# A macaron block on one NeuronCore: the attention output product as three fp32r passes, its input split on ScalarE and VectorE, and the bias sums on GpSimd moved

## The reference

```python
x = x + 0.5 * ffn(norm(x))          # first half step
x = x + attn(norm(x))               # RWKV time mix and channel mix
x = x + 0.5 * ffn(norm(x))          # second half step
# ffn: weighted sum of 8 chosen 256x256 adapters and their biases
# inside attn, on its own input a:
h = layernorm(a, ln1);  hh = h shifted by one token
xk, xv, xr = h * tm + hh * (1 - tm)
k, v, sr = xk @ Wk.T, xv @ Wv.T, sigmoid(xr @ Wr.T)
rwkv = sr * wkv(time_decay, time_first, k, v)   # a scan over tokens
a = a + rwkv @ Wo.T                              # the output product
h = layernorm(a, ln2);  hh = h shifted by one token
kk = square(relu(xck @ Wck.T))                   # keys, 1024 wide
a + sigmoid(xcr @ Wcr.T) * (kk @ Wcv.T)          # gate times values
```

## Time and profile before

| what | value |
|---|---|
| median of 3 runs | 431.5 us (431.36 to 431.73) |
| the profiled execution | 431.73 us, span 429.9 us |
| TensorE matmul busy | 417.1 us, 97% |
| TensorE weight loads busy | 337.0 us, 78% |
| VectorE busy | 367.9 us, 86% |
| ScalarE busy | 329.7 us, 77% |
| GpSimd busy | 185.6 us, 43% |
| granted TensorE clock | 1.000 over the span |

### The profile page before, as it was taken

How to read it: one execution, slowest core, us unless ns; L and a number is a source line. 1 busy time by engine, 2 the same in 40 slices (tenths; PEclk the granted TensorE clock), 3 DMA queues, 4 the chain that set the end, 5 groups by cost and what they waited for, 6 DMA issues and landing times.

```text
span 429.9 us, 6308 instructions
## 1 busy us (share of the span) xinstructions
PE 417.1 (97%) x2042; PEld 337.0 (78%) x2042; DVE 367.9 (86%) x725; ACT 329.7 (77%) x669; POOL 185.6 (43%) x194
## 2 busy tenths in 40 slices
PE   8989989889999999999999999999999999999996
PEld 8865875568868887798769886888779876988985
DVE  2988989998989999998989998999999898886235
ACT  1157977899799969997899979997999489945420
POOL 1446052727272635635372728263553347033011
PEclk9999999999999999999999999999999999999999
DMA  6992010001000110002000200010000000000101
GB/s 200 376 398 81 2 49 0 0 2 52 0 0 2 57 44 0 0 26 74 2 0 25 74 1 2 0 50 1 2 0 25 26 0 2 25 26 0 50 2 50
DMA packets 15972, 18.52 MB, mean 43 GB/s; under 512 B 1083, under 2 KB 13635, under 8 KB 15939
## 3 DMA queue, kind: packets, MB, share of 16 engines
q1 hardware_dynamic: 14538, 17.05, 11.4%
q10 hardware_dynamic: 1400, 1.07, 0.8%
HBM read 13.92 MB, written 4.19 MB: 42 GB/s over the span
## 4 chain that ended last, share of the span: by engine, by line
PE 77%; DVE 1%; issue 0%; ACT 0%; DVEq 0%
PE pair L484 22%; PE pair L362 10%; PE pair L374 10%; PE pair L458 6%; PE pair L459 6%; PE pair L462 6%; PE pair L352 6%; PE pair L343 4%; PE pair L499 3%; PE pair L428 1%; PE pair L432 1%; PE pair L429 1%; PE pair L514 0%; DVE rwkv L1054 0%; DVE work L1048 0%
## 5 line engine op out<-in xcount | busy, mean ns | idle before, releaser
L484 PE MATMUL pair<-wcv_sb,kk 128*128 128x256 f32 x448 | 100.4, 380 | 0.0
L484 PEld LDWEIGHTS pair<-wcv_sb,kk 128*128 128x128 f32 x448 | 83.8, 190 | 11.3 <-ACT kk L741 0.7
L458 PE MATMUL pair<-xck_hi,wck_hi 128*128 128x512 f32 x128 | 54.4, 425 | 0.0
L462 PE MATMUL pair<-xck_lo,wck_hi 128*128 128x512 f32 x128 | 50.7, 396 | 0.0
L459 PE MATMUL pair<-xck_hi,wck_lo 128*128 128x512 f32 x128 | 50.6, 395 | 0.0
L737 ACT ACTIVATE kk<-pair 128x512 f32<-128x512 f32 x64 | 36.3, 589 | 14.2 <-PE pair L462 13.3
L1349 POOL TENSOR_TENSOR x2b<-xs,bias_bc 128x512 f32<-128x512 f32 (+1 forms) x16 | 21.8, 1364 | 56.6 <-DVE xcr_lo L1127 22.9
L1349 POOL TENSOR_TENSOR x<-x,bias_bc 128x512 f32<-128x512 f32 x14 | 18.1, 1296 | 55.7 <-DVE rwkv L1054 36.3
L741 ACT ACTIVATE kk<-kk 128x512 f32<-128x512 f32 x64 | 35.9, 625 | 0.0
L1389 POOL TENSOR_TENSOR xs<-x,xa 128x512 f32<-128x512 f32 x16 | 20.4, 1273 | 31.6 <-DVE xa L1060 31.0
L1309 POOL TENSOR_TENSOR rstd_x<-vare_x,nhalf 128x4 f32<-128x4 f32 (+2 forms) x26 | 27.3, 1050 | 9.1 <-DVE vare_x L909 7.8
(11 more groups left out here) (173 smaller groups left out, 1119.3 us busy)
## 6 DMA issues: line engine op xcount, KB each, us to landing
x<-in_x_dram SPq DMA_DIRECT2D x8, 512.0 KB, 4.0
out_dram<-xs SPq DMA_DIRECT2D x15, 256.0 KB, 2.1
xt<-in_xt_dram SPq DMA_DIRECT2D x4, 512.0 KB, 8.2
work<-in_ffn_w_dram ACTq DMA_DIRECT2D x4, 256.0 KB, 5.1
work<-in_ffn_w_dram SPq DMA_DIRECT2D x4, 256.0 KB, 5.2
kk<-in_wck_dram SPq DMA_DIRECT2D x1, 1024.0 KB, 9.6
xs<-in_xt_dram SPq DMA_DIRECT2D x2, 512.0 KB, 10.8
wcv_sb<-in_wcv_dram SPq DMA_DIRECT2D x1, 1024.0 KB, 12.5
```

Of the source, the lines that this page charges most:

```text
L458: nc.tensor.matmul(key_bank(n), wck_hi[:, h, cols], xck_hi[:, h, :], start=h == 0, stop=False)
L462: last = nc.tensor.matmul(key_bank(n), wck_hi[:, h, cols], xck_lo[:, h, :], start=False, stop=h == CH - 1)
L484: last = nc.tensor.matmul(bank_of("kv", e, i)[:, t % TB * C:(t % TB + 1) * C], kk[:, n, tok:tok + P], wcv_sb[:, n, :], start=n == 0, stop= ...
```

## The change

For batches 1 to 7 the output product runs through `three_passes`. Its weight is split once at the start (`wo_hi`, `wo_lo`), its input for each batch: `rwkv_hi` is a copy on ScalarE, `rwkv_lo` a difference on VectorE. TensorE now waits for `rwkv_lo` and not for `rwkv`, and the product stands behind six of the eight matmuls of `channel_values(e, 0)` in place of four. On ScalarE the copies stand behind square 5, the residual behind them, then squares 6 and 7, and the channel gate last. On VectorE the two differences stand around the first half of `add_second`. On GpSimd the two sums into `x1` both wait for the denominators (`den_done`) and no longer for the scan `aa` and for `rwkv`. Of the sums into `x2b`, the one that stood first waits for `xcr_lo`, and the other moves to the end of the iteration before, behind `xcr`. The values of the last batch (`last_values`) are three passes as well, with their keys and weight split.

```diff
             def output_product(f):
                 if f == 0:
                     pe.wait_ge(s_wo, 1)
-                pe.wait_ge(rwkv_done, 2 * f + 2)
-                to_tokens("o", rwkv, wo_sb, xa2_done, f, o_ps)
+                    pe.wait_ge(rwkv_done, 2 * f + 2)
+                    to_tokens("o", rwkv, wo_sb, xa2_done, f, o_ps)
+                    return
+                if f == 1:
+                    pe.wait_ge(s_wo_lo, 1)
+                pe.wait_ge(rwkv_lo_done, 2 * (f - 1) + 2)
+                for i in range(BANKS):
+                    take(pair_of("o", f), i, xa2_done, 2 * f + i + 1)
+                    for t in range(TB):
+                        last = three_passes(bank_of("o", f, i)[:, t * C:(t + 1) * C], i * TB + t, rwkv_hi, rwkv_lo, wo_hi, wo_lo)
+                    last.then_inc(o_ps, 1)
...
                 for n in part:
+                    high = wcv_hi[n // (HB // 2)][:, n % (HB // 2), :]
                     if t == 0:
-                        pe.wait_ge(sq_done, HB * LAST + n + 1)
-                    last = nc.tensor.matmul(by_tiles(last_bank(LAST_KV, j), j)[:, t - LAST_PARTS[j][0], :], kk[:, n, t * P:(t + 1) * P], wcv_sb[:, n, :],
-                                            start=n == 0, stop=n == HB - 1)
+                        pe.wait_ge(kk_hi_done, n + 1)
+                    nc.tensor.matmul(dst, kk_hi[:, n, tok], high, start=n == 0, stop=False)
+                    nc.tensor.matmul(dst, kk_hi[:, n, tok], wcv_lo[:, n, :], start=False, stop=False)
+                    if t == 0:
+                        pe.wait_ge(kk_lo_done, n + 1)
+                    last = nc.tensor.matmul(dst, kk_lo[:, n, tok], high, start=False, stop=n == HB - 1)
...
-                channel_values(e, 0, range(HB // 2))
+                channel_values(e, 0, range(HB - 2))
                 if has(f):
                     output_product(f)
-                channel_values(e, 0, range(HB // 2, HB))
+                channel_values(e, 0, range(HB - 2, HB))
...
+            def output_input_high(f):
+                act.wait_ge(r_ps, 2 * f + 2)
+                for h in range(CH):
+                    act.wait_ge(rwkv_done, 2 * f + h + 1)
+                    nc.scalar.activation(rwkv_hi[:, h, :], rwkv[:, h, :], ACT.Copy).then_inc(rwkv_hi_done, 1)
...
+            def output_input_rest(f, h):
+                dve.wait_ge(rwkv_hi_done, 2 * (f - 1) + h + 1)
+                nc.vector.tensor_tensor(rwkv_lo[:, h, :], rwkv[:, h, :], rwkv_hi[:, h, :].bitcast(F32), ALU.subtract).then_inc(rwkv_lo_done, 1)
...
+                if has(f):
+                    output_input_rest(f, 0)
                 if has(e - 1):
                     add_second(e - 1, 0)
+                if has(f):
+                    output_input_rest(f, 1)
...
                 if has(e - 1):
+
+                    pool.wait_ge(xcr_lo_done, 2 * e + 2)
                     bias_to_x2(e - 1, 1)
                 if e - 1 >= SUMS_X2:
                     inverse_std("x2", e - 1)
-                if has(e - 1):
-
-                    pool.wait_ge(xcr_lo_done, 2 * e + 2)
-                    bias_to_x2(e - 1, 0)
...
-                    pool.wait_ge(aa_done, 2 * f + 2)
+                    pool.wait_ge(den_done, 2 * f + 2)
                     bias_to_x(f + 1, 0)
-                    pool.wait_ge(rwkv_done, 2 * f + 2)
                     bias_to_x(f + 1, 1)
```

More of the change, by code:

```diff
@@ L148, in build @@
         rwkv = sb("rwkv", [P, CH, T])
+        rwkv_hi, rwkv_lo = in_place_of("xr", "rwkv_hi", [P, CH, T]), in_place_of("rwkv", "rwkv_lo", [P, CH, T])
         xv_hi, xv_lo = in_place_of("thr", "xv_hi", [P, CH, T]), in_place_of("xv", "xv_lo", [P, CH, T])
@@ L381, in ffn_setup @@
                 pe.wait_ge(s_bias_sel, 16 * K)
-                nc.tensor.matmul(pair[0][:, 0, 0:C], gate_rows[:, :], bias_sel[:, :], start=True, stop=True).then_inc(s_bias_ps, 1)
+                nc.tensor.matmul(pair[0][:, 0, 0:C], gate_rows[:, :], bias_sel, start=True, stop=True).then_inc(s_bias_ps, 1)
                 pe.wait_ge(s_ffn_acc, K)
@@ L385, in ffn_setup @@
                     for h in range(CH):
-                        last = nc.tensor.matmul(pair[0][:, 1, a * C:(a + 1) * C], (centre_own if a == h else centre_other)[:, :], ffn_sum[:, h, :],
+                        last = nc.tensor.matmul(pair[0][:, 1, a * C:(a + 1) * C], (centre_own if a == h else centre_other), ffn_sum[:, h, :],
                                                 start=h == 0, stop=h == CH - 1)
@@ L874, in _ @@
                     key_square(e, n)
+                for n in range(HB // 2, HB - 2):
+                    key_square(e, n)
+                if has(f):
+                    output_input_high(f)
+                    residual_of(f)
+                for n in range(HB - 2, HB):
+                    key_square(e, n)
                 channel_gate(e)
[L876 to L879, removed]
                 if has(f + 1):
@@ L888, in _ @@
                     past_cr(f)
+            key_relu(LAST, 4)
+            for n in range(HB - 5):
+                last_key_parts(n)
+                key_relu(LAST, n + 5)
+            for n in range(HB - 5, HB):
+                last_key_parts(n)
+            channel_gate(LAST)
             for j in range(len(LAST_PARTS)):
@@ L1174, in last_bias, with last_weight_rest, last_key_rest @@
                                         bias_bc[:, :].rearrange("p (a c) -> p a c", a=1).broadcast_to([P, len(LAST_PARTS[j]), C]), ALU.add).then_inc(x2b_parts[j], 1)
+            def last_weight_rest():
+                dve.wait_ge(s_wcv, 2)
+                for i in range(2):
+                    some = slice(i * HB // 2, (i + 1) * HB // 2)
+                    last = nc.vector.tensor_tensor(wcv_lo[:, some, :], wcv_sb[:, some, :], wcv_hi[i][:, :, :].bitcast(F32), ALU.subtract)
+                last.then_inc(s_wcv_lo, 1)
+            def last_key_rest(n):
+                dve.wait_ge(kk_hi_done, n + 1)
+                dve.wait_ge(sq_done, HB * LAST + n + 1)
+                nc.vector.tensor_tensor(kk_lo[:, n, :], kk[:, n, :], kk_hi[:, n, :].bitcast(F32), ALU.subtract).then_inc(kk_lo_done, 1)
             def add_second(e, i):
@@ L1255, in _ @@
                     wkv_gated(f)
-                elif has(e - 1):
+                else:
                     second_rest(e - 1)
+                    last_weight_rest()
+                    for n in range(HB // 2):
+                        last_key_rest(n)
+                if has(f):
+                    output_input_rest(f, 0)
                 if has(e - 1):
                     add_second(e - 1, 0)
+                if has(f):
+                    output_input_rest(f, 1)
                 if has(f + 1):
@@ L1270, in _ @@
                 if e == LAST:
+                    for n in range(HB // 2, HB):
+                        last_key_rest(n)
                     break
```

54 lines of the change are left out of this document (45 added, 9 removed).

## The result

The changed kernel takes 440.95 us (median of 4 runs, 440.73 to 441.35) against 431.5: a ratio of 1.0217, 95% interval 1.0204 to 1.0231. The profiled execution is 440.73 us with a span of 438.9, so 9.0 us more than before inside the span.

A forecast was written before the change was run, and what follows sets the result against it. TensorE, busy 97%, was taken to set the time, with VectorE's `rwkv` only 0.5 us ahead. Losses 7.5 + 1.1 + 0.6 less 2.3 gave 6.9 us on 431.73, so 438.6, forecast 438.4; range 431.5 to 441.

The forecast's parts named there:

- this mechanism for itself: Main forecast, scan held and split chain making the product wait: 438.4 us, own range 436.5 to 440.5, chance 0.58.
- the 441 that bounded all the cases: Upper end of the overall range 431.5 to 441, which left out the second rival and the heavy case.
- The passes: Output products: three fp32r passes at 0.117 us each save 0.080 us a matmul, 0.64 us a product.
- The end part: Last batch's values in three passes: 2.55 us shorter, 0.2 lost at the first turning with the load, so -2.3 us.
- The split chain: ScalarE copies and VectorE differences before the output product: `rwkv_lo` ready about 2.15 us after `rwkv`.
- The hold: GpSimd's sum into `x1` holds VectorE's second `aa` scan 1.05 us; `rwkv` ends 0.9 later, the product starts 2.59 later.
- The rival in which the scans are not held: GpSimd sums do not hold VectorE's scans: 432.2 us, up to 433.5 if the turnings wait longer; chance 0.17.
- the one in which the sums leave VectorE's chain: The 1.05 us freed at `xk` reaches `rwkv`, none is put back: 427.4, or 424.9 without turning waits; chance 0.12.
- the idle microsecond before `x2t_lo`: VectorE: the 1.05 us freed at `xk` becomes waiting before `x2t_lo`, which needs `x2t_hi`; gain costed at nothing.
- The turning: `turn_xa` on TensorE waits 0.3 us for normed tiles; with it an iteration loses 1.5 us, five lose 7.5.
- e = 0: First output product: no `add_second` between the copies and differences, starts at 97.5 in place of 95.25; 1.1 us lost.
- e = 6: Output product with no sum for a next batch left: starts 1.68 us late, 0.6 us lost.

The follow-up runs named there:

- the third experiment: Kernel before with only the GpSimd sums moved as in the change, the output product plain: 435.49 us, ratio 1.0087.
- the fourth: Changed kernel with the second difference of `rwkv` ahead of `add_second` instead of behind it: 438.49 us, ratio 1.0139.
- second experiment: Kernel before with only the last batch's values in three passes, with the key and weight splits they need: 429.81 us, ratio 0.9942.
- seventh experiment: Changed kernel with eight identity products issued on TensorE while it waits for the product of e = 0: 440.09 us, ratio 1.0196.
- first: Changed kernel with the two GpSimd sums into `x1` waiting for `aa_done` and `rwkv_lo_done`; forecast 434.6, measured 438.72 us, ratio 1.0151.
- tenth: Changed kernel without the splits of `rwkv` and its weight, three passes over other ready operands, output not the block's: 429.91 us, ratio 0.9956.
- sixth: Changed kernel, `x1` sums at iteration start and `aa_done`, second difference ahead of `add_second`, turning four matmuls later; forecast 426, measured 438.23 us, ratio 1.0156.
- ninth: Changed kernel, `x1` sums at iteration start and `aa_done`, second difference ahead of `add_second`, turning left in place: 432.53 us, ratio 1.0018.
- The eleventh: Changed kernel, second difference ahead of `add_second`, turning two matmuls later, `x1` sums a batch ahead beside the norm and at `aa_done`: 427.90 us, ratio 0.9909.
- the twelfth: The eleventh with first-half `add_second` behind the output sum and the turning one matmul after tile 2's start, not two: 429.40 us, ratio 0.9945.
- eighth: Changed kernel with only the turning of `xa` four matmuls later: 438.57 us, ratio 1.0170.

## Why the prediction held, step by step

It forecast 438.4 us, slower for a hold on the scans and a split chain ahead of the product. Both are there, in those places: the third experiment has the hold by itself, and the fourth takes 0.78 us out of the chain. It was 2.5 us short: 440.95 lies 0.45 above the 436.5 to 440.5 that I gave this mechanism for itself, and only just inside the 441 that bounded all the cases. The error is mostly e = 0, and there mostly a cost that was not in the sum at all.

- **The passes.** 0.117 us a matmul was right (0.12 here). The product takes 2.97 us, saving 0.48; with the restart counted (0.11) I had 0.53. The end part gave 2.23 for 2.3, and alone 2.2 (second experiment).
- **The split chain.** `rwkv_lo` 2.23 us behind `rwkv`, for 2.15.
- **The hold.** 1.07 us on the second scan, for 1.05; the product started 2.66 later than before, for 2.59. The rival in which the scans are not held is out, by the changed kernel and by the third experiment. So is the one in which the sums leave VectorE's chain: the idle microsecond before `x2t_lo` is where the prediction put it. The Trainium skill, SBUF — State Buffer, Who interferes with whom, says that a VectorE instruction with two SBUF inputs and a GpSimd one that reads SBUF shut each other out; with the scans, `xk`, `add_first` and `xv_lo` the traces agree. By its words the loser waits for the whole instruction; 0.96 to 1.07 us is what a sum that takes 1.27 costs here (`xv_lo`, which met `xr`, lost 1.2).
- **The turning.** 0.4 us of wait for 0.3. With it an iteration lost 1.72 us for 1.5, five of them 8.6 for 7.5.
- **e = 0.** 2.87 lost for 1.1, the term that was off most. Half of it, 1.46 us, is the granted clock after the 2.24 us of rest. The prediction had the wait (2.25 us by its numbers) and not what followed on the clock; without the fall the product takes 2.92 (seventh experiment). The other 1.4 is for 1.1: the product comes 2.44 later for 2.28, and the turning waits 0.4.
- **e = 6.** 0.65 for 0.6.
- 7.5 + 1.1 + 0.6 - 2.3 = 6.9 became 8.6 + 2.9 + 0.6 - 2.2 = 9.9, less the 0.85 of an earlier start: 9.0. That earlier start is luck of this execution: it hides a part of the error.

What the prediction did not see is how the costs hang together. I had treated `add_first` as work that nobody waits for: with the product earlier it is what `xa` waits for (first, fourth and tenth experiments). And with nobody waiting for the split, but the hold on the scan left in, the product's passes win nothing, because the turning takes their gain (tenth). My forecast of 434.6 failed on the first point. The one of 426 failed on the later turning, which pushed VectorE's next round back (sixth and ninth). The eleventh, where turning, differences and sums are all moved, does gain: some 1.5 us beside the last values' 2.2, from 46.36 to 46.2 in an iteration. Up to the product of e = 6, where TensorE idles nowhere ahead of it, the distance is 45.8, so about 0.4 an iteration are left.

Open stays what bounds the eleventh. Its chain runs through ScalarE (tanh, squares, `rwkv_hi`) into the product, while VectorE too has little rest; the twelfth moved the wait from the one place to the other and does not tell which of them would have to be shortened. Why the clock fell in two profiles after the same rest and not in a third (below) is open as well; the run times of the fourth and eighth kernels look as if it changed from one execution to the next.

## What to carry to other kernels

A faster matmul in the middle of a ring of engines is worth what the next wait leaves of it: add up the time from the operand's last producer to the next point at which TensorE needs a result, and price the split of the operands there. A GpSimd sum of 1.27 us costs VectorE about 1 us where it meets one of VectorE's instructions with two SBUF inputs; put it where VectorE is idle anyway or reads PSUM, and look again after each other edit, since idle time that hides a hold goes when anything upstream moves. A part of the change that stands at the end, with no ring behind it, should be timed by itself: here it was all that the change gained.

## What the runs showed of the hardware

- VectorE's scan with two SBUF inputs is held by a GpSimd sum like any other such operation, 1.06 to 1.07 us.
- A TENSOR_SCALAR on float32 in SBUF with one data input is held too, four of them 2.34 us for 1.38. The Trainium skill, SBUF — State Buffer, Who interferes with whom, does name `tensor_scalar` among the operations that can take the shared ports in a fast mode; the eleventh experiment agrees.
- After 2.24 us of rest TensorE's granted clock went from 2.4 to 1.2 GHz when the next work was under way, 1.0 us into it in the changed kernel and 0.4 in the fourth, and back 3.4 us later. It did not in the eighth with the same rest of 2.23 us, nor in any profile after rests of 1.3 to 1.8 us. In the fourth and eighth kernels two of four runs have a mean granted clock of 0.994 or 0.995 and are 0.8 to 2.4 us longer, and a fall of 3.4 us takes 0.004 off that mean. That would fit a fall in some executions of one kernel and not in others; it is not shown, since one execution of each was profiled.
